# A three-stage mixture kernel on one core: router weights in one run a partition, a prologue in a new order, and routing weights that are never multiplied out

## What is computed

```python
def _L0_ffn_ref(x, A, B, Wr):          # K = 64 experts of rank 16, the best 16 of each row
    scores = xf @ Wr.T
    top_vals, top_idx = jax.lax.top_k(scores, TOPK)
    gates = jax.nn.softmax(top_vals, axis=-1)
    G = jnp.zeros((N, K), xf.dtype).at[jnp.arange(N)[:, None], top_idx].set(gates)
    h = jnp.einsum('nd,krd->nkr', xf, A)
    out = jnp.einsum('nkr,kdr->nd', h * G[:, :, None], B)
    return (out * SCALING).reshape(*prefix, -1)

def _L0_attn_ref(x, w_gate, w_up, w_down):      # I = 1376
    s = jax.nn.silu(jnp.einsum('bsh,ih->bsi', x, w_gate))
    # ... the half of each row of s with the smallest |s| is set to zero
    s = s * jnp.einsum('bsh,ih->bsi', x, w_up)
    return jnp.einsum('bsi,hi->bsh', s, w_down)

x = x + 0.5 * _L0_ffn_ref(_layernorm(x, axis=-1), L0_ffn_A, L0_ffn_B, L0_ffn_Wr)
x = x + _L0_attn_ref(_layernorm(x, axis=-1), L0_attn_w_gate, L0_attn_w_up, L0_attn_w_down)
x = x + 0.5 * _L0_ffn_ref(_layernorm(x, axis=-1), L0_ffn_A, L0_ffn_B, L0_ffn_Wr)
```

## Time and profile before

| | us |
|---|---|
| median of 3 runs | 705.83 (705.51 to 705.92) |
| the profiled execution | 706.07 |
| its span in the trace | 704.3 |
| TensorE busy | 689.8 (98%) |
| VectorE, ScalarE, GpSimd busy | 471.7, 359.6, 217.9 |

### The profile page before, as it was taken

How to read it: one execution, slowest core, us unless ns; L and a number is a source line. 1 busy time by engine, 2 the same in 40 slices (tenths; PEclk the granted TensorE clock), 3 DMA queues, 4 the chain that set the end, 5 groups by cost and what they waited for, 6 DMA issues and landing times.

```text
span 704.3 us, 10405 instructions
## 1 busy us (share of the span) xinstructions
PE 689.8 (98%) x3699; PEld 333.9 (47%) x3699; DVE 471.7 (67%) x984; ACT 359.6 (51%) x467; POOL 217.9 (31%) x545
## 2 busy tenths in 40 slices
PE   4999999999999999999999999999999999999998
PEld 3444444444444444544445444444444444444445
DVE  6899776866585666647666576566746565738863
ACT  5788876525545253462525545254453445676210
POOL 4122435424324042341423315142240424444000
PEclk9999999999999999999999999999999999999999
DMA  9977414245434162543414434242442415123453
GB/s 323 290 194 204 63 16 87 51 81 102 77 72 97 38 96 52 99 77 50 98 30 102 75 66 89 45 95 45 87 76 34 84 30 102 31 56 72 77 93 82
DMA packets 171867, 62.28 MB, mean 88 GB/s; under 512 B 163648, under 2 KB 163904, under 8 KB 171808
## 3 DMA queue, kind: packets, MB, share of 16 engines
q1 hardware_dynamic: 171808, 61.56, 41.7%
HBM read 16.97 MB, written 4.19 MB: 30 GB/s over the span
## 4 chain that ended last, share of the span: by engine, by line
PE 74%; POOL 7%; ACT 6%; issue 5%; DVE 5%; DMA 2%; SPq 0%; DVEq 0%; POOLq 0%; ACTq 0%
PE ps L616 14%; PE ps L617 14%; PE ps L618 14%; PE ps L733 10%; PE ps L737 10%; PE ps L734 10%; ACT signs L967 5%; POOL small L535 2%; POOL small L532 2%; POOL small L531 1%; DMA mem<-w_a 1%; POOL small L533 1%; DMA xt_f<-halves 1%; DVE mem L1356 1%; DVE tops L1358 1%
## 5 line engine op out<-in xcount | busy, mean ns | idle before, releaser
L967 ACT ACTIVATE signs<-mem,small 128x1376 bf16<-128x1376 f32 x112 | 161.4, 1441 | 152.9 <-POOL small L535 135.6
L616 PE MATMUL ps<-w_a_hi,xt_f 128*128 128x512 f16 x248 | 94.0, 379 | 0.0
L618 PE MATMUL ps<-w_a_lo,xt_f 128*128 128x512 f16 x248 | 94.0, 379 | 0.0
L734 PE MATMUL ps<-w_b_lo,pt_hi 128*128 128x512 f16 x248 | 94.0, 379 | 0.0
L617 PE MATMUL ps<-w_a_hi,xt_f 128*128 128x512 f16 x248 | 94.0, 379 | 0.0
L733 PE MATMUL ps<-w_b_hi,pt_hi 128*128 128x512 f16 x248 | 94.0, 379 | 0.0
L491 POOL TENSOR_SCALAR rvar<-mv 128x1 f32<-128x1 f32 x48 | 11.4, 238 | 186.6 <-DVE mv L1211 185.1
L616 PE MATMUL ps<-w_g_hi,xt 128*128 128x512 f16 (+1 forms) x192 | 68.5, 357 | 0.2 <-DVE mem L1327 0.2
L618 PE MATMUL ps<-w_g_lo,xt 128*128 128x512 f16 (+1 forms) x192 | 68.5, 357 | 0.0
L617 PE MATMUL ps<-w_g_hi,xt 128*128 128x512 f16 (+1 forms) x192 | 68.5, 357 | 0.0
L618 PE MATMUL ps<-w_u_lo,xt 128*128 128x512 f16 (+1 forms) x192 | 68.5, 357 | 0.0
(11 more groups left out here) (152 smaller groups left out, 1225.1 us busy)
## 6 DMA issues: line engine op xcount, KB each, us to landing
x<-x SPq DMA_DIRECT2D x14, 256.0 KB, 3.4
out<-x SPq DMA_DIRECT2D x13, 256.0 KB, 2.3
mem<-w_g SPq DMA_DIRECT2D x4, 688.0 KB, 12.5
mem<-w_u SPq DMA_DIRECT2D x4, 688.0 KB, 5.6
mem<-w_d SPq DMA_DIRECT2D x5, 512.0 KB, 6.2
mem<-w_a SPq DMA_DIRECT2D x4, 512.0 KB, 6.1
mem<-w_b SPq DMA_DIRECT2D x4, 512.0 KB, 9.0
pt_hi<-p_hi SPq DMA_TRANSPOSE x32, 3.2
```

The source lines that it names most:

```text
L616: pe.matmul(dst, x_hi, w_hi, start=start, stop=False)
L618: return pe.matmul(dst, x_hi, w_lo, start=False, stop=stop)
L734: pe.matmul(dst, x_hi[:, c, :], lo[m.name][:, c, :], start=False, stop=False)
L967: act.activation(signs[:, :], mags[h], ACT.Sign, bias=thr[h], scale=-1.0, accum_out=bal[h]).then_inc(counted[h], 1)
```

## The change

**Router weights.** Matrix r is laid out on the host so that each partition's 4 x 64 values are one run of 256; it is loaded by one DMA with 128 runs instead of 4 x 128.

**Routing weights.** The multiplication that made `weight` is gone, and with it the tile. `apply_route` multiplies by 1/sum (one value a partition) and by `chosen` in one instruction, `p_to_hi` multiplies by GATE_S, and `p_to_lo` computes `routed` times GATE_S minus `p_hi`.

**Order of the prologue.** Each engine's list is rearranged up to the first trip of the loop; the loop and the tail keep their order. TensorE also gets 6 unused matmuls after each of the first three pieces of a's norms and 12 after the fourth, and 6 in place of 16 in the first call of `experts`.

```diff
@@ load_w @@
+                    if m is MR:
+                        sp.dma_start(mem[:, m.at:m.at + DC * KE], dram["r"]
+                                     ).then_inc(w_loaded["r"][0], 16)
+                        continue
@@ SP @@
-            load_w(MG, 0, 1, 2, 3)
-            load_x(4)
+            load_w(MG, 0, 1)
             turn_x(1, 2)
-            load_u(0)
+            load_w(MG, 2)
             turn_p_hi(0)
             turn_x(1, 3)
+            load_w(MG, 3)
+            turn_p_lo(0)
+            load_x(4)
+            load_u(0)
+            turn_p_hi(1)
             load_u(1)
-            turn_p_lo(0)
+            load_x(5)
+            turn_p_lo(1)
             load_u(2)
-            turn_p_hi(1)
-            load_x(5)
             load_x(6)
-            turn_p_lo(1)
             load_u(3)
             turn_p_hi(2)
             turn_x(1, 4)
@@ GpSimd @@
             rstd(2, 1)
+            aim(0)
             rstd(2, 2)
-            aim(0)
+            search(0, 0)
             make_scale(MD)
-            search(0, 0)
             search(0, 1)
@@ TensorE @@
-                    busy(16)
+                    busy(6)
...
-            norms(MA)
+            for n in range(len(MA.pieces)):
+                norms(MA, n, n + 1)
+                busy(6 if n < len(MA.pieces) - 1 else 12)
...
             combine(1, 1)
+            experts(1, 4)
             pe.wait_ge(scale_made, 4)
             norms(MU)
-            experts(1, 4)
             combine(1, 2)
@@ ScalarE @@
             square(MR, 0)
             square(MA, 0)
+            square(MA, 1)
             turned_to_hi(0)
+            square(MA, 2)
+            square(MA, 3)
             split_hi(MR, 0)
-            for n in range(1, len(MA.pieces)):
-                square(MA, n)
...
-            for n in range(len(MU.pieces)):
-                square(MU, n)
+            square(MU, 0)
+            square(MU, 1)
             split_hi(MG, 0)
+            square(MU, 2)
+            p_to_hi(3)
             split_hi(MG, 1)
-            p_to_hi(3)
+            square(MU, 3)
             x_to_hi(2, 0)
...
             tanh(0)
-            p_to_hi(4)
             square(MD, 3)
             square(MD, 4)
             magnitude(0)
+            p_to_hi(4)
@@ VectorE: route, apply_route, p_to_lo @@
-                link(dve.tensor_scalar(weight[:, :], chosen[:, :], inv_total, GATE_S,
-                                       ALU.mult, ALU.mult))
...
+                dve.scalar_tensor_tensor(
+                    out=routed[:, :].rearrange("p (k r) -> p k r", r=RANK),
+                    in0=bank(banks_of(k), KR).rearrange("p (k r) -> p k r", r=RANK),
+                    scalar=inv_total, in1=chosen[:, :].unsqueeze(2).to_broadcast([P, KE, RANK]),
+                    op0=ALU.mult, op1=ALU.mult).then_inc(routed_ready, 1)
...
+                dve.scalar_tensor_tensor(out=p_lo[:, :], in0=routed[:, :], scalar=GATE_S,
+                                         in1=p_hi[:, :], op0=ALU.mult, op1=ALU.subtract
+                                         ).then_inc(p_lo_ready, 1)
@@ VectorE @@
             norm_stats(1, 4)
+            split_lo(MB, 2)
+            split_lo(MB, 3)
             p_to_lo(1)
-            split_lo(MB, 2)
             route(2)
-            split_lo(MB, 3)
             apply_route(2)
             norm_apply(1, 4)
             read_scores(3)
             choose(3)
             p_to_lo(2)
+            read_norm(MG)
             x_to_lo(1, 4)
...
             route(4)
-            apply_route(4)
             split_lo(MU, 2)
             silu(0)
+            apply_route(4)
             split_lo(MU, 3)
```

More of the change, by code:

```diff
@@ L1023, in _ @@
             square(MB, 0)
+            square(MB, 1)
             x_to_hi(1, 2)
-            for n in range(1, len(MB.pieces)):
-                square(MB, n)
+            square(MB, 2)
+            square(MB, 3)
             exps(0)
@@ L1279, in apply_route_last @@
                     dve.wait_ge(of, at)
-                    dve.tensor_tensor(
-                        routed[:, halves_of[h]].rearrange("p (k r) -> p k r", r=RANK),
-                        bank(banks_of(k) + h).rearrange("p (k r) -> p k r", r=RANK),
-                        weight[:, heads[h]].unsqueeze(2).to_broadcast([P, KE // 2, RANK]),
-                        ALU.mult).then_inc(done, 1)
+                    dve.scalar_tensor_tensor(
+                        out=routed[:, halves_of[h]].rearrange("p (k r) -> p k r", r=RANK),
+                        in0=bank(banks_of(k) + h).rearrange("p (k r) -> p k r", r=RANK),
+                        scalar=inv_total,
+                        in1=chosen[:, heads[h]].unsqueeze(2).to_broadcast([P, KE // 2, RANK]),
+                        op0=ALU.mult, op1=ALU.mult).then_inc(done, 1)
             def p_to_lo(k):
@@ L1475, in _ @@
             square_right(0)
+            square_right(1)
+            square_right(2)
             turned_to_lo(0)
-            split_lo(MR, 0)
-            square_right(1)
-            make_unscale(unscale_r, "r")
-            square_right(2)
             square_right(3)
@@ L1483, in _ @@
             norm_stats(1, 1)
+            split_lo(MR, 0)
+            make_unscale(unscale_r, "r")
+            norm_stats(1, 2)
             read_scores(0)
-            norm_stats(1, 2)
+            norm_apply(1, 1)
             split_lo(MA, 0)
-            norm_apply(1, 1)
             split_lo(MA, 1)
             split_lo(MA, 2)
-            norm_apply(1, 2)
             split_lo(MA, 3)
             turned_to_lo(1)
+            norm_apply(1, 2)
+            choose(0)
             x_to_lo(1, 2)
-            choose(0)
             norm_stats(1, 3)
@@ L1523, in _ @@
             norm_stats(2, 0)
-            read_norm(MG)
             route(3)
@@ L1528, in _ @@
             split_lo(MG, 0)
-            read_norm(MU)
             p_to_lo(3)
@@ L1533, in _ @@
             add_ffn(1, 1)
+            read_norm(MU)
             norm_stats(2, 1)
@@ L1560, in _ @@
             add_ffn(1, 3)
-            norm_stats(1, LEAD)
             dve.wait_ge(thr_ready[0], 2)
             p_to_lo(4)
+            norm_stats(1, LEAD)
             x_to_lo(2, 2)
@@ L1709 @@
         "x": x.reshape(B * S, D),
-        "w_r": np.ascontiguousarray(np.transpose(inputs["L0_ffn_Wr"])),
+        "w_r": np.ascontiguousarray(np.transpose(np.transpose(inputs["L0_ffn_Wr"]).reshape(
+            D // P, P, K), (1, 0, 2)).reshape(P, D // P * K)),
         "w_a": np.ascontiguousarray(np.transpose(np.reshape(a, (K * R, D)))),
```

20 lines of the change are left out of this document (6 added, 14 removed).

## The result

The changed kernel takes **708.69 us** (median of 6 runs, 707.74 to 709.67), the kernel before beside it 705.88 (705.42 to 707.44). The ratio is 1.0039, 95% interval 1.0026 to 1.0052: about 2.8 us slower, where 2.0 faster was forecast. The profiled execution took 708.78 with a span of 707.0 (before: 706.07 and 704.3). VectorE is busy for 465.5 us instead of 471.7, so the removed multiplications are gone, and the time is not.

A forecast was written before the change was run, and what follows sets the result against it. TensorE was taken to bound the kernel, busy for 98% of the span. The terms 2.1 + 0.17 - 0.1 = 2.15 on 706.07 gave 703.9, or 703.7 in a median; forecast 703.8, range 702.8 to 705.3.

The forecast's parts named there:

- Router layout, 0.15 us: Loading r in one run at the start: a's last piece lands 0 to 0.24 us earlier, taken as 0.15.
- The first call: Prologue, call 0: the experts' matmuls start between 13.6 and 13.9 us, as before.
- The clock rises by 14.2: Call 0: filled gaps raise TensorE's clock by 14.2 us, the cold rest costs 0.2, and call 1 starts at 19.75.
- Rival 1: Call 0: the clock rises when it did before, call 2 starts at 26.15, 704.4 us results; chance 0.22.
- Call 2 starts 2.1 us earlier: Prologue: tile 2's transpose lands at 25.35, so call 2 starts at 25.4 instead of 27.51.
- Who is late next: 0.1 us: Prologue after call 2: VectorE's splits and the transposes of tiles 3 and 4 all fit; 0.1 us deducted.
- Rival 3: Call 4: tile 4's transpose meets loads of u, TensorE idles 4.8 us, 708.6; chance 0.09, of which 0.05 slower.
- Call 4's lo half, 0.17 us: Call 4: GpSimd's first search step comes before d's scale, so TensorE's 0.17 us wait for the lo half goes.
- The second search, rival 2: Second search: GpSimd's steps fall worse by 1 to 1.5 us, TensorE waits at 131, 705 to 705.3; chance 0.09.
- Routing weights, 0: From 140 us on and in the tail: 32 instructions of 0.25 us leave VectorE, worth 0 there.
- The sum: Whole kernel: 2.1 + 0.17 - 0.1 = 2.15 us gained on 706.07.

The follow-up runs named there:

- b_r_new: The kernel before with the router's new layout of r alone; ratio 1.0000.
- b_filler: The kernel before with the new unused matmuls alone (6, 6, 6 and 12 between the norms, 6 before the experts); ratio 1.0005.
- b_weights: The kernel before with the change's routing weights alone; 706.42 us beside 704.95, ratio 1.0018.
- a_sp_pad: The changed kernel with SyncE's old prologue list and two unused VectorE operations ahead of tile 14's second-half subtraction (v_to_lo); 706.20 us, ratio 1.0010.
- a_sp_old: The changed kernel with SyncE's prologue list of the kernel before, all else as changed; 706.34 us, ratio 1.0022.

## Why the prediction was wrong

The forecast was 703.8 with 0.05 for slower; the result is 708.7. Point by point:

- **Router layout, 0.15 us.** No gain that can be told (b_r_new 1.0000, interval 0.6 us either way; 0.15 is inside it). The moment at which a's last piece lands is 10.45 in before's profile, 11.07 after, and 11.15 in b_r_new, 11.08 in b_filler. I took 10.45 as this kernel's; it was the earliest of the seven kernels that start from before.
- **The first call.** Every step of the chain from a's last piece was as worked out, but 0.8 us late with it, plus 0.25 for `w_r_lo`: the experts start at 14.85, not at 13.6 to 13.9.
- **The clock rises by 14.2.** It did at about 18.2, later than before's 16.2. Eight matmuls ran 0.21 us slow each, 1.7 us where I had put 0.2. Rival 1 was right on this. VectorE was in time (a's lo splits end at 19.9, tile 1's turned lo half at 20.5), so TensorE's own sum holds, 19.6 + 1.05 + 1.5, and call 1 starts at 22.13 instead of 19.75. This is the first step that failed.
- **Call 2 starts 2.1 us earlier.** It starts at 27.76, 5.63 us after call 1 as worked out; the 2.4 us that it misses are call 1's. The transpose of tile 2 went as predicted (issued 22.94, landed in 3.1 us, no wait). Besides, 1.36 of the gain was counted from before's idle time, a wait of 1.22 us that comes and goes: b_filler and b_r_new, whose lists on SyncE are before's, don't have it (transposes of 4.9 and 5.2 us, call 2 at 27.09 and 26.94), b_weights has 0.62 and a_sp_pad 1.69. Over all profiles with SyncE's old list call 2 starts at 26.6 to 27.8, with the new one at 27.0 to 28.5, and at 26.1 to 27.1 with tile 4 early. I took one execution's wait for the kernel's.
- **Who is late next: 0.1 us.** This step cost the sign. I checked when tile 4's *halves* would be ready, and not when tile 4 itself would be loaded, though I had written that its load was moved. VectorE's statistics of tile 4 at 35.5 waited for a load issued at 32.12, which was behind `turn_p_lo(0)`, hence behind VectorE's first `p_lo`. I had the transpose issued at 45.3 and landed at 48.5; it was issued at 47.87 and landed at 53.4, and TensorE waited 1.74 us. Rival 3 had the transpose among loads and the price, 708.6, but I held against it that the loads of u would be issued by 42 and through by 45.5. They went out at 43.5 to 44.6, since SyncE issues them behind `turn_p_lo(1)`. My rows dated the loads by the old times, although the instruction ahead of them was 3.7 us later, 2.4 of it by the splits of b that I had moved ahead myself. Its chance should have been several times 0.05. That its 708.6 lies beside the 708.7 measured is luck: it had 4.8 us of idle time from a transpose of 8.7, the trace has 1.74 from one of 5.5, and the rest came from elsewhere.
- **Call 4's lo half, 0.17 us.** It came: from call 4's combination to its lo half are 3.45 us (83.50 to 86.95), 3.62 before. It was lost again in the search: at call 5 after is 1.98 us behind before, at stage 3's first call 2.11.
- **The second search, rival 2.** A lead is lost, but one search earlier: of a_sp_old's lead of 0.89 us 0.41 went between 93 and 106 us. A long GpSimd step has a part in it, as the rival had it: `make_scale(MD)` takes 1.60 us for 0.57. That the new list puts it between two search steps I had not priced.
- **Routing weights, 0.** The durations were right (`p_lo` 1.22, `apply_route` 1.28 for 1.22), the conclusion was not: 0.97 us in the trace, 1.3 (0.6 to 1.8) by b_weights. I looked for who waits for VectorE and not for whom VectorE holds up, though the earlier trace rows had GpSimd's step of 1.80 us before my eyes.
- **The sum.** The terms add up to 2.17, not 2.15; it changes nothing.

## What to carry to other kernels

A load moved behind an instruction that waits starts when that wait ends, and so does everything listed behind it: follow the moved load to its *first* reader, and date each later transfer by the new time of what SyncE waits for. Don't count a wait as the kernel's own until a second execution or a neighbouring kernel shows it. On a chain of small GpSimd steps that TensorE waits for, any shift of VectorE by some tenths counts, so a change that removes VectorE work needs a look at what now runs beside those steps. And two waits that add up to the loss are not yet its account: add up the starts of the calls, where gains show too.
